# Reordering the first 46 microseconds of a residual MLP with per-row experts on one Trainium2 core

## What is computed

```
h = gelu(x @ fc1_w.T + fc1_b)                     # (32, 256, 1024)
shared = h @ fc2_w.T + fc2_b                      # 192 outputs
expert_x = h @ experts_w[idx].T + experts_b[idx]  # 64 outputs, one expert per row
out = x + concatenate([shared, expert_x], axis=-1)
```

## Time and profile before

| | |
|---|---|
| median of three runs | 364.22 us (364.06 to 364.25) |
| the profiled execution, device time | 364.22 us |
| the profiled execution, span | 362.4 us |
| PE busy in the span | 354.1 us (98%) |
| DVE, ACT, POOL busy | 62%, 67%, 62% |

### The profile page before, as it was taken

The page is one execution under the profiler, slowest core; times in us unless marked ns, Lnnn a source line. Parts: engine busy times, 40 slices in busy tenths (PEclk is TensorE's granted clock), DMA queues, the critical chain, the costliest instruction groups (busy, mean ns, idle before and its releaser), DMA issues.

```text
span 362.4 us, 7783 instructions
## 1 busy us (share of the span) xinstructions
PE 354.1 (98%) x2833; PEld 348.4 (96%) x2833; DVE 223.8 (62%) x367; ACT 243.5 (67%) x410; POOL 223.1 (62%) x100
## 2 busy tenths in 40 slices
PE   4999999999999999999999999999999999999996
PEld 3889899999999999999999999999999999999996
DVE  1697993947749385682937658295673938653341
ACT  3694866757949577695757849576694857757560
POOL 0079914775656776565676656677565677655381
PEclk9999999999999999999999999999999999999999
DMA  8879856261513516134361614426052321403011
GB/s 200 180 157 120 176 140 176 82 163 35 148 59 101 141 52 172 48 108 104 91 151 45 166 33 126 115 71 170 31 145 68 91 92 55 130 15 103 0 60 58
DMA packets 70448, 37.86 MB, mean 104 GB/s; under 512 B 43531, under 2 KB 70411, under 8 KB 70411
## 3 DMA queue, kind: packets, MB, share of 16 engines
q1 hardware_dynamic: 69792, 36.85, 40.1%
q10 hardware_dynamic: 618, 0.53, 0.6%
HBM read 28.97 MB, written 8.39 MB: 103 GB/s over the span
## 4 chain that ended last, share of the span: by engine, by line
PE 93%; issue 2%; POOL 1%; DMA 1%; ACT 1%; ACTq 0%; DVE 0%; POOLq 0%
PE fc_ps L977 37%; PE acc_ps L1009 16%; PE acc_ps L1013 16%; PE acc_ps L1011 16%; PE fc_ps L953 6%; POOL ht L351 1%; DMA w_in<-in_L_cond_fc_w 1%; PE fc_ps L960 1%; PE acc_ps L922 1%; ACTq L234 0%; ACT ht L508 0%; PE tr_ps L922 0%; ACT gelu L534 0%; DVE work L792 0%; DVE resid L817 0%
## 5 line engine op out<-in xcount | busy, mean ns | idle before, releaser
L351 POOL TENSOR_TENSOR ht<-gelu,ht 128x1024 fp32r<-128x1024 f32 x60 | 144.5, 2409 | 122.6 <-ACT ht L508 122.6
L977 PE MATMUL fc_ps<-xt,w1t 128*128 128x256 f32 x1176 | 173.2, 284 | 0.0
L977 PEld LDWEIGHTS fc_ps<-xt,w1t 128*128 128x128 f32 x1176 | 155.3, 192 | 0.1
L1009 PE MATMUL acc_ps<-w2t,ht 128*128 128x256 f32 x512 | 145.1, 283 | 0.2 <-POOL ht L351 0.2
L1013 PE MATMUL acc_ps<-w2t,ht 128*128 128x256 f32 x512 | 145.1, 283 | 0.0
L1011 PE MATMUL acc_ps<-w2t,ht 128*128 128x256 f32 x512 | 145.1, 283 | 0.0
L1009 PEld LDWEIGHTS acc_ps<-w2t,ht 128*128 128x128 f32 x512 | 98.4, 192 | 0.6 <-POOL ht L351 0.3
L1011 PEld LDWEIGHTS acc_ps<-w2t,ht 128*128 128x128 f32 x512 | 98.4, 192 | 0.3
L1013 PEld LDWEIGHTS acc_ps<-w2t,ht 128*128 128x128 f32 x512 | 98.4, 192 | 0.0
L508 ACT ACTIVATE ht<-gelu 128x1024 fp32r<-128x1024 f32 x64 | 68.0, 1062 | 3.3
L494 ACT ACTIVATE work<-fc_ps 128x512 f32<-128x512 f32 x28 | 16.7, 598 | 57.4 <-PE fc_ps L977 57.4
(11 more groups left out here) (55 smaller groups left out, 274.5 us busy)
## 6 DMA issues: line engine op xcount, KB each, us to landing
pieces<-in_L_cond_experts_w SPq DMA_DIRECT2D x128, 64.0 KB, 2.0
out<-resid SPq DMA_DIRECT2D x32, 256.0 KB, 2.8
pieces<-in_x SPq DMA_DIRECT2D x60, 128.0 KB, 3.6
resid<-in_x SPq DMA_DIRECT2D x15, 512.0 KB, 4.1
bias<-in_L_cond_experts_b SPq DMA_DIRECT2D x32, 32.0 KB, 3.0
w_piece<-in_L_cond_fc_w SPq DMA_DIRECT2D x4, 256.0 KB, 4.5
w_piece<-in_L_cond_fc_w SPq DMA_DIRECT2D x4, 192.0 KB, 5.0
resid<-in_x SPq DMA_DIRECT2D x2, 256.0 KB, 3.6
```

Of the source, the lines that this page charges most:

```text
L351: nc.gpsimd.tensor_tensor(ht[:, slot, LO, :, :].rearrange("p k t -> p (k t)"), gelu[:, q % GELUS, :, :].rearrange("p k t -> p (k t)"), ht[ ...
L977: last = nc.tensor.matmul(fc1_ps[:, dst, j * SEQ:(j + 1) * SEQ], w1t[:, w, wv, ms], xt[:, n % 2, o, xv, :], start=(fresh and j == 0 and at ...
L1009: nc.tensor.matmul(dst, h_hi_t, w_hi, start=(r == 0 and u % (2 * T) == 0), stop=True, skip_group_check=True)
```

## The change

It touches the program of every engine, up to the beginning of block 2; the loop over blocks 2 to 15 stays as it is.

- SP: block 0 of x is one transfer of 512 KB, and nothing waits behind it; `load_x_pieces(2)` goes from ahead of the experts of block 1 to behind `load_w1_pieces`.
- PE: `warm` issues matmuls of the identity, read as bf16, into a bank that nobody reads: 20 as soon as the identity is made, and 10 more after the transposes of x. The transposes of x are grouped by feature half over all four tiles.
- DVE: the second-layer weights start ahead of the low parts of the second half of the first-layer weights. `x_square(2)` and all that hangs on it (`x_sums_*`, `x_low`) go behind the first `s_square`, `plain_low(4)` and `s_low(0)`. `plain_low(6)` and the two drains of block 0 change places with other steps.
- ACT: the same steps in an order to match.
- POOL: `x_sums_lo(2)` goes from ahead of the weight sums to behind `residual(0)`.

```diff
--- before.py
+++ after.py
@@ -5,6 +5,7 @@
 
 FP32 = mybir.dt.float32
 FP32R = mybir.dt.float32r
+BF16 = mybir.dt.bfloat16
 ALU = mybir.AluOpType
 ACT = mybir.ActivationFunctionType
 
@@ -32,6 +33,7 @@
     PAIRS = K // 2
     BANK = 512
     GELUS = 4
+    WARM = 20
 
 
 
@@ -110,7 +112,6 @@
                     for n in range(PLAIN)]
         xt0 = xt_plain[0]
 
-        x0_loaded = [sem(f"x0_loaded{b}") for b in range(R)]
         x_loaded = [sem(f"x_loaded{n}") for n in range(2)]
         xp_loaded = [sem(f"xp_loaded{n}") for n in range(2)]
         e_loaded = [sem(f"e_loaded{n}") for n in range(2)]
@@ -279,11 +280,7 @@
                                  .rearrange("p q k j -> p (q k) j"), w1_pieces[q])\
                         .then_inc(w1p_loaded, 16)
 
-            for b in range(R):
-                ts = slice(b * T, (b + 1) * T)
-                sp.dma_start(resid[:, 0, ts, :], x_blocks[0][:, ts, :]).then_inc(x0_loaded[b], 16)
-
-            sp.wait_ge(x0_loaded[0], 16)
+            load_x(0)
             load_w1(sp, 1)
             for q in range(Q):
                 sp.dma_start(w2_piece[S * q:S * (q + 1), :, :], w2_v[q]).then_inc(w2_loaded, 16)
@@ -291,9 +288,9 @@
             numbers = load_experts(0)
             load_x_pieces(1)
             load_expert_bias(0, numbers)
-            load_x_pieces(2)
             numbers = load_experts(1)
             load_w1_pieces()
+            load_x_pieces(2)
             sp.dma_start(
                 bias[:, :, :, 0:SHARED].rearrange("p a b o -> p (a b) o"),
                 fc2_b.rearrange("(o c n) -> o c n", o=1, c=1).to_broadcast([P, 2 * R, SHARED]))\
@@ -334,11 +331,7 @@
         def _(pool):
             def residual(n):
                 par = n % 2
-                if n == 0:
-                    for b in range(R):
-                        pool.wait_ge(x0_loaded[b], 16)
-                else:
-                    pool.wait_ge(x_loaded[par], 16 * ((n + 1) // 2))
+                pool.wait_ge(x_loaded[par], 16 * (n // 2 + 1))
                 pool.wait_ge(be_loaded[par], 16 * R * (n // 2 + 1))
                 rows = resid[:, par, :, :].rearrange("p (b t) d -> p b t d", b=R)
                 nc.gpsimd.tensor_tensor(
@@ -380,7 +373,6 @@
 
             for r in range(PAIRS):
                 pair_lo(r)
-            x_sums_lo(PLAIN)
             pool.wait_ge(w1p_loaded, 16 * Q)
 
             pool.wait_ge(w1_tr, 2 * D)
@@ -394,6 +386,7 @@
 
             pool.wait_ge(x0_tr, D)
             residual(0)
+            x_sums_lo(PLAIN)
             residual(1)
             for n in range(PLAIN, BLOCKS):
                 for g in range(GROUPS):
@@ -573,9 +566,9 @@
             act.wait_ge(b1_ready, 1)
             conv_chunk(0)
             w1_high(1, 0)
+            w2_high(0)
+            conv_chunk(1)
             w1_high(1, 1)
-            conv_chunk(1)
-            w2_high(0)
             w2_high(1)
             conv_chunk(2)
             w2_high(2)
@@ -592,24 +585,24 @@
                 x1_high(d)
             conv_chunk(7)
             conv_high(2)
-            b_copy(PLAIN)
-            x_high(PLAIN)
+            conv_high(3)
 
             conv_chunk(8)
-            conv_high(3)
-            x_sums_high(PLAIN)
             conv_chunk(9)
             conv_high(4)
             experts_high(1, 0)
             s_high(0)
             conv_chunk(10)
+            b_copy(PLAIN)
+            x_high(PLAIN)
             conv_chunk(11)
             conv_high(5)
+            conv_chunk(12)
+            x_sums_high(PLAIN)
             s_high(1)
-            s_high(3)
-            conv_chunk(12)
             conv_chunk(13)
             conv_high(6)
+            s_high(3)
             s_high(2)
             conv_chunk(14)
             conv_chunk(15)
@@ -822,12 +815,12 @@
                 w1_low(0, d)
             dve.wait_ge(b1_tr, 1)
             nc.vector.tensor_copy(b1[:, :], fc1_ps[:, 3, 0:K]).then_inc(b1_ready, 1)
-            for d in range(D):
-                w1_low(1, d)
             w2_square(0)
             w2_square(1)
+            w1_low(1, 0)
             w2_low(0)
             w2_square(2)
+            w1_low(1, 1)
             w2_low(1)
             w2_square(3)
             w2_low(2)
@@ -844,33 +837,33 @@
                 x1_low(d)
 
             dve.wait_ge(x1_lo, D)
+            experts_square(1, 0)
+            s_square(0)
+            plain_low(4)
+            experts_low(1, 0)
+            s_low(0)
+            dve.wait_ge(e_lo, 3)
+            dve.wait_ge(s_lo, 1)
             for d in range(D):
                 x_square(PLAIN, d)
+            plain_low(5)
             x_sums_first(PLAIN)
             x_low(PLAIN, 0)
             x_sums_last(PLAIN)
             x_low(PLAIN, 1)
             dve.wait_ge(xb_lo, 2)
             dve.wait_ge(t_added, 4)
-            experts_square(1, 0)
-            plain_low(4)
-            s_square(0)
-            experts_low(1, 0)
-            s_low(0)
-            dve.wait_ge(e_lo, 3)
-            dve.wait_ge(s_lo, 1)
             s_square(1)
             s_square(3)
-            plain_low(5)
+            plain_low(6)
             s_low(1)
             s_low(3)
+            drain(0, 0)
+            drain(0, 1)
             dve.wait_ge(s_lo, 3)
             s_square(2)
             experts_square(1, 1)
             s_low(2)
-            drain(0, 0)
-            drain(0, 1)
-            plain_low(6)
             plain_low(7)
 
             for n in range(PLAIN, BLOCKS):
@@ -922,14 +915,15 @@
                     last = nc.tensor.transpose(dst[:, c * P:(c + 1) * P], tile, ident[:, :])
                 return last
 
-            def x0_banks(b):
-                pe.wait_ge(x0_loaded[b], 16)
-                for d in range(D):
-                    last = transposes(tr_ps[:, d, b * SEQ:(b + 1) * SEQ],
-                                      [feature_chunk(resid[:, 0, b * T + t, :], d)
-                                       for t in range(T)])
-                    if b == R - 1:
-                        last.then_inc(x0_tr, 1)
+            def warm(times):
+                bits = ident[:, :].bitcast(BF16)
+                for _ in range(times):
+                    nc.tensor.matmul(fc1_ps[:, 2, 0:2 * P], bits[:, 0:P], bits,
+                                     start=True, stop=True)
+
+            def x0_bank(d):
+                transposes(tr_ps[:, d, :], [feature_chunk(resid[:, 0, t, :], d)
+                                            for t in range(TILES)]).then_inc(x0_tr, 1)
 
             def w1_bank(half, d):
                 transposes((acc_ps, tr_ps)[half][:, d, :], [
@@ -1018,8 +1012,11 @@
                         last.then_inc(acc_filled, 1)
 
             pe.wait_ge(ident_ready, 1)
-            for b in range(R):
-                x0_banks(b)
+            warm(WARM)
+            pe.wait_ge(x_loaded[0], 16)
+            for d in range(D):
+                x0_bank(d)
+            warm(WARM // 2)
             pe.wait_ge(w1_loaded[0], 16 * Q)
             for d in range(D):
                 w1_bank(0, d)
```

## The result

| | before | after |
|---|---|---|
| median of the runs | 364.24 us (4 runs, 364.06 to 364.75) | 374.83 us (4 runs, 374.12 to 375.15) |
| ratio | | 1.0286 (95% interval 1.0267 to 1.0305) |
| profiled execution, span | 364.22 us, 362.4 us | 375.64 us, 373.9 us |

The changed kernel is slower by 10.6 us. The direction was forecast (371.1 us), the size was not: the time lies outside the range of 368.0 to 373.5 us.

What follows compares the result with a forecast made beforehand. The prediction took PE as the bound, with no idle time from 12.4 us on. It added p7's 6.9 us delay in block 2 to 364.2 us, giving 371.1 us, range 368.0 to 373.5 us.

Steps and rivals of the forecast that it cites:

- The hole: After p1 of block 2, PE waits for `drain(0, 0)`, which ends at 49.2 us: 4.25 us idle.
- the second and third steps: In block 2, p2 starts at 52.35 instead of 46.72 us, then p7 at 59.75 instead of 52.83 us.
- the sum: Step-by-step chain through DVE, ACT and PE to p7 of block 2, 6.9 us late, giving 371.1 us.
- The two waits of DVE on ACT: Ahead of the drain, DVE idles for `conv_high(5)` and `conv_high(6)`, 2.3 and 1.6 us.
- Rival (a): The drain ends by 45.0 us, PE never waits, and the head's gain stands alone: 363.6 us; chance 0.07.
- DVE: `plain_low` 1.7 us beside POOL, bound 2.13: On DVE, `plain_low(4)` and `plain_low(6)` take 1.7 us beside POOL; 1.23 alone, 2.13 at most.
- Landing 8.2 us, chunk 1 at 12.1 us: In the head, weights land at 8.2 instead of 7.06 us; chunk 1 starts at 12.1 instead of 12.4 us.
- the forecast's 48.45 us: On DVE, two `s_low` end at 48.45 us, and `drain(0, 0)` of 0.75 us follows.
- Edits at no cost: Later `load_x_pieces(2)` and `x_sums_lo(2)` cost nothing; POOL's weight pieces are there by 25 us, wanted at 29.7.
- (b): In the head, warm matmuls at a low clock delay the weight transposes by 1.5 us: 372.6 us; chance 0.08.
- (c): The clock falls in PE's 4.25 us wait, and matmuls take about twice their time: 371.9 us; chance 0.15.

Runs made afterwards that it cites:

- Numbers 6: The changed kernel with `plain_low(5)` moved to where `plain_low(6)` stood and `plain_low(6)` to just ahead of `plain_low(7)` on DVE: 367.59 us, ratio 1.0106.
- number 9: The changed kernel with only `plain_low(6)` moved on DVE, to directly ahead of `plain_low(7)`: 372.8 us, ratio 1.0215.
- 10: The changed kernel with only `plain_low(5)` moved on DVE, to directly ahead of `plain_low(6)`: 369.89 us, ratio 1.0164.
- Number 7: The changed kernel with `residual(1)` on POOL moved behind `x_sums_lo(3)`: 372.98 us, ratio 1.0230.
- Number 5: The changed kernel with 45 more warm matmuls on PE right after p1 of block 2: 375.03 us, ratio 1.0284.
- number 2: The changed kernel with SP waiting for block 0 of x before issuing its half of the first-layer weights: 374.92 us, ratio 1.0289.
- number 11: The kernel before with warm matmuls in three parts (11, 3, 4), plus the new middle order with both `plain_low` moved back: 367.09 us, ratio 1.0074.
- numbers 12: The changed kernel with both `plain_low` moved back and block 2's work on x ahead of the first `s_square` again: 366.94 us, ratio 1.0068.
- 14: The 366.94 us kernel (both `plain_low` back, work on x first) with the drains behind the last `s_square`, `s_high(3)` still late: 366.53 us, ratio 1.0057.
- number 1: The changed kernel with the middle order undone on DVE, ACT, POOL and SP, only the head staying changed: 365.11 us, ratio 1.0023.

## Why the direction was right and the size wrong

**What bounds it, and where the loss comes from: right.** The hole stands after p1 of block 2 and is ended by the drain; the second and third steps (p2 behind the GELUs, p7 behind `add_v`) follow as written. From p2 to p7 it took 7.3 us where the sum had 7.4. The two waits of DVE on ACT were 2.50 and 1.75 us against 2.3 and 1.6. Numbers 6, 9 and 10 show that these two places decide: without them 6.6 of the 10.6 us are gone. Rival (a) fell by this.

**"DVE: `plain_low` 1.7 us beside POOL, bound 2.13": wrong, the step that failed first.** I took the longest of a few rows as the bound of a slowdown. It is a wait with a known end (POOL's end + 1.08 us), so its bound is the length of POOL's instruction, 2.4 us, plus 1.08, less the lag: 3.5 us if both start together. `plain_low(6)`, with a lag of 0.17 us, measured 3.26 against 1.7, `plain_low(5)` 1.97 against 1.24, together 2.3 us. The rows of before would have told it, had I set DVE's ends beside POOL's ends. Number 7 confirms the size: 2.04 us off the instruction, 1.9 us off the kernel.

**"Landing 8.2 us, chunk 1 at 12.1 us": wrong.** The landing was 10.07 us in the profiled execution; the sharing of the rate cost 3.0 us and not 1.15. The clock rose early, at 4.4 us (from there on a warm matmul takes 273 ns instead of 417), but PE then idled for 2.75 us and it fell back for `first_chunk`. Chunk 1 was 3.2 us later than forecast (15.3 against 12.1), and `s_square(0)` 2.4 us (33.69 against 31.3). Between the two, POOL ended `pair_lo(3)` 3.0 us late (32.67 against 29.7) and gained 0.5 us: its first weight sum took 1.04 us, where I had 1.56 from a row in which DVE was busy. In the trace this is the other half of the miss: 2.4 + 2.3 = 4.7 us, against 4.65 us measured at the drain (53.10 against 48.45 us), and p7 11.4 us late against 6.9.

**That second half is not a cause by itself.** The experiments correct the account from the trace, whose head was unusually late. Number 5 has the same order up to the drain; there the weights landed at 9.35 us, the clock stayed up, and chunk 1 started at 13.31 us and `s_square(0)` at 31.76 us, 0.5 us after the forecast. The drain is still 4.1 us after the forecast's 48.45 us. POOL's row, then DVE's:

```profile
39.77 3.02 POOL L337 TENSOR_TENSOR resid<-resid,bias 128x1024 f32<-128x1024 f32 x1 [2.90 <-DMA bias<-in_L_cond_fc_b]
```

```profile
39.31 1.23 DVE L720 TENSOR_TENSOR ht<-gelu,ht 128x1024 fp32r<-128x1024 f32 x1 [2.50 <-ACT ht L501]
40.45 2.63 DVE L715 TENSOR_TENSOR work<-b_rows 128x256 f32<-128x256 f32 x1
...
48.23 3.24 DVE L720 TENSOR_TENSOR ht<-gelu,ht 128x1024 fp32r<-128x1024 f32 x1 [1.74 <-ACT ht L501]
```

`residual(0)`, which the forecast had nowhere on the path, holds the first sum of x (2.63 us, alone 0.41), and `residual(1)` holds `plain_low(6)`: 2.2 + 1.5 = 3.7 of the 4.1 us are POOL's hold. That the other runs of the changed kernel went this way is likely (their mean granted clock is 0.989 to 0.991, that of the profiled one 0.985) and not shown.

With the head as forecast (number 2) the time stays, because **"Edits at no cost"** fails in its place: the pieces for POOL were said to be there by 25 us and landed at 31.0 us in number 2 and 29.8 in number 11, as SP issues them only at 23.56 us, behind the experts of block 1. And the second-layer bias, issued behind them, came at 40.9 us, so that `residual(0)` fell on the work on x. POOL's wait for the pieces is 1.03 us there; how the loss of number 2 divides between the pieces and the bias, no run shows. In the changed kernel itself the pieces were in time, and the bias was 0.92 us late. I had closed that paragraph with "if one of them were late, the chain above would grow by that lateness", and did not look at SP's timeline of the kernel before, where the issue stands at 24.69 us:

```profile
24.69 2.81 SPq L278 DMA_DIRECT2D w_piece<-in_L_cond_fc_w  x4
```

So with the head as forecast it is a transfer and no longer compute that starts the chain: `s_square(0)` at 32.1 us in number 2, against 31.3 in the forecast, and then the hold of POOL on top.

**Rivals.** (b), the warm matmuls in the way, did not happen: the clock was up at 4.4 us, before the first 20 ended at 5.28 us. (c), the clock falling in the wait, happened: the granted clock is 0.84 and 0.75 in the two stretches above. Its price of 0.8 us was too high, for number 5 finds none. The Trainium skill ("TensorE: Matmul & The Clock Gate", "Why this matters for your kernels") was right that the clock falls in such a gap; what it costs depends on whether PE is what is waited for. Here it was not; in number 9 it was, and the low clock cost 1.3 us.

**A third wait on ACT that the forecast did not have.** The sum let `s_low(3)` follow at once. In the changed kernel it does, because DVE stands at `plain_low(6)` until then; when that step is away, the wait for `s_high(3)` comes to light (1.46 us in number 9, 3.2 us in numbers 12 and 14).

**The account of 10.6 us** (10.4 by the ratios), each line taking the one before as its start: the two `plain_low` to their old places 6.6 us (1.0286 to 1.0106); the work on x ahead of the weight sums 1.4 us (to 1.0068; the two intervals overlap); `s_high(3)` ahead of chunk 12 1.3 us (to 1.0032); what is left of the middle 0.3 us (to 1.0023, number 1, within the error); the head 0.8 us. The order matters: in number 2, with all four in place, a repaired head gave nothing.

## What to carry over

An in-order engine's step that waits for another engine is to be placed behind everything that is ready and that others wait for; a step put early "so that it is done" (here `plain_low(5)` and `plain_low(6)` in front of the drain) delays all of that by its wait. Where two engines exclude each other, price a step as the end of the other's instruction plus its own rest, read from paired ends in the trace, never as an average or as the longest of its durations. And before counting on an earlier start, look when the queue engine issues what this start needs.
